# A fused layer on one core: the first stage's small adds and the feed-forward's factors are laid out anew over the engines

## The chip, the cores and the metric

The kernel runs on one core of one Trainium2 chip. The metric is the device time of one execution in microseconds (us), the median of several runs. The engines are called TensorE (PE; its weight loads are PEld), VectorE (DVE), ScalarE (ACT), GpSimd (POOL) and the sync queue (SP), which issues all transfers.

## The reference

For x of 2048 rows by 512, x plus an attention and a feed-forward, both of the normalized x:

```python
xn = (x - mean(x)) / sqrt(var(x) + 1e-5)
q = xn @ wq                       # 16 heads of 128 + 64
kva = xn @ wkv_a                  # 128 latents, 64 rotary key columns
ckv = kva[:, :128] * rsqrt(mean(kva[:, :128]**2) + 1e-6) * kv_norm_scale
k_nope, v = ckv @ wkv_b           # per head 128 and 128
scores = (concat(q_nope, rope(q_pe)) . concat(k_nope, rope(k_pe))) * 192**-0.5   # causal
attn = softmax(scores) @ v @ wo
mixed = sum_r(xn @ factors[r]) / sqrt(8) + bias    # 8 factors of 512x512
out = x + attn + mixed
```

## The kernel before

Every product is done in three matmuls of 16-bit high and low parts (`three`, L387 to L390). There are 16 row tiles of 128 rows (`NT`), 8 pairs of them (`NP`), 4 chunks of 512 queries (`NC`), and 64 units (`NU`): a chunk with a head each, the last chunk first. A unit has four rows r (query tiles); chunk 3, which the first 16 units work on, has four pieces of up to 512 keys per row.

Each engine has its own program in fixed order; semaphores bind them.

**First stage**, a loop over t = 0 to 19. On TensorE (L603 to L623): transpose of x tile t (`transpose_x`), some weight transposes, at odd t from 5 on `keys((t-5)/2)` (L475), which transposes a pair's scaled latents and turned rotary keys, `q_rope(0)` at t = 17 and `q_latent(0)` at t = 18, then `latent_product(t-2)`. On VectorE (L1203 to L1239), at even t from 4 on, `latent(p)` (L1043): the reciprocal (L1052), the rotary products out of the accumulator banks (L1055, L1058) into `kt` and `ktmp`, and the adds of the two halves (L1063), 128x128 each, two per pair. Later in the same t `value_parts` (L1066) subtracts the high part of the latents (128x256, L1069). It also takes the low parts of x, keys, absorbed weights, and the statistics of x. ScalarE (L822 to L857) normalizes, copies high parts, squares and takes roots; it scales the latents into `kt`, which has two buffers. GpSimd (L1334 to L1339) adds the eight factors into `fsum`, 28 adds of 128x512 in fixed order (`factor`, L1255), each when its tile has landed in one of four landing buffers, then scales some weights, adds the rotary halves of unit 0's queries (`q_rope`, L1295) and makes their low parts (`rope_parts`, L1309).

The sync queue is in order too (L1495 to L1530): x pairs, weights, 4 + 4 factor tiles, the rest of x, bias, table, then eight rounds of three factor tiles, where a load waits until GpSimd has used its buffer. In round 4 it also issues heads 2 and 3's weights; `load_wp(2)` waits for VectorE's `w_pe(0)` (L1022).

**Units.** TensorE writes a row's scores (L535 to L541; the rotary products L540, L541 wait for GpSimd's parts), VectorE takes the maxima (L1114, L1116) and the scaled negative maximum `nm` (L1132), ScalarE the exponentials (L769) and their high parts (L779), GpSimd the low parts (L1318), and a transposing transfer brings them to TensorE for the product with the latents. Between rows every engine does what the list `fills(i, r)` (L92) gives for this unit and row, each its own share of it. In unit 0 that list has: the query product of unit 1, the squares and norm of the factors (`sqf`, `nf`), their scaling to 16-bit parts (`factors_high` L811 on ScalarE, `factors_low` as the end of `scale_factors`, L971, on VectorE), and then all 8 feed-forward tiles, four in row 2 and four in row 3 (12 matmuls each). VectorE adds each tile into the residual (L1086) once GpSimd has added the bias to it (`add_bias`, L1276; two, three and three of them behind rows 0, 1 and 2).

```python
    if i == 0 and r >= 2:
        out += [("ffn", n) for n in range((r - 2) * QT, (r - 1) * QT)]
```

Small tiles of products rotate over four accumulator banks in the first stage and over three in the units (`bank_order`, L177): a use waits for the previous reader of its bank.

## Time and profile before

| | |
|---|---|
| median of 3 runs | 1557.49 us (1557.07 to 1558.05) |
| profiled execution, own time | 1555.18 us |
| its span | 1553.2 us |
| TensorE busy | 1483.4 us (96%) |
| VectorE busy | 1074.2 us (69%) |
| ScalarE busy | 971.6 us (63%) |
| GpSimd busy | 893.2 us (58%) |

The profile shows one execution. Times in it count from the span's start. A busy share over the whole span mixes the first stage (to about 85 us) with the 64 units, so the table by stage is to be read before the shares.

### The profile page before, as it was taken

To read this page: it belongs to the slowest core of one execution; us is meant where nothing else is said; L and a number is where in the kernel's file an instruction comes from. 1 tells how busy PE (TensorE), PEld (TensorE's weight loads), DVE (VectorE), ACT (ScalarE), POOL (GpSimd) and SP (SyncE) were. 2 spreads that over 40 slices of the span, in tenths; PEclk is the share of its full clock that TensorE was granted. 3 is DMA by queue.
4 is the path that set the end of the run, shared out by engine and by line. 5 is a ranking of instruction groups with operands and counts; after the bars stand their busy time and mean duration, and the time that the engine had idled before them with its cause. 6 is when DMAs were issued, how large, how long until landed. Compare 5 with 4: busy or idle time off the path is not lost.

```text
span 1553.2 us, 25687 instructions
## 1 busy us (share of the span) xinstructions
PE 1483.4 (96%) x7908; PEld 759.2 (49%) x7908; DVE 1074.2 (69%) x2534; ACT 971.6 (63%) x2409; POOL 893.2 (58%) x881
## 2 busy tenths in 40 slices
PE   4669999999999999999999999999999999999997
PEld 4534454545454455444454444544545555454543
DVE  6855778777877776665565655566766666686887
ACT  6654767677677767656666666665646665554554
POOL 3564566565556565656656565656646565564553
PEclk9979999999999999999999999999999999999999
DMA  8645777878777789878786777887856667754454
GB/s 274 193 115 118 152 158 137 162 154 166 151 153 155 139 152 195 154 130 168 144 164 138 135 142 144 150 166 130 180 129 133 136 139 151 153 127 98 107 127 106
DMA packets 646886, 229.93 MB, mean 148 GB/s; under 512 B 599392, under 2 KB 612192, under 8 KB 646112
## 3 DMA queue, kind: packets, MB, share of 16 engines
q1 hardware_dynamic: 646752, 228.30, 71.4%
q8 instruction: 65, 1.06, 0.3%
q14 instruction: 69, 0.57, 0.1%
HBM read 66.72 MB, written 18.87 MB: 55 GB/s over the span
## 4 chain that ended last, share of the span: by engine, by line
PE 83%; issue 5%; DVE 5%; ACT 4%; POOL 2%; DMA 1%; SPq 1%; DVEq 0%; ACTq 0%; POOLq 0%
PE ps L388 16%; PE ps L389 16%; PE ps L390 16%; PE ps L535 7%; PE ps L540 7%; PE ps L541 7%; PE ps L536 7%; PE ps L537 7%; ACT ex L769 2%; POOL early L1265 1%; DVE gm L1114 1%; DVE acc L1166 1%; DVE ps L1116 1%; DVE tot L900 0%; ACT wV L736 0%
## 5 line engine op out<-in xcount | busy, mean ns | idle before, releaser
L1318 POOL TENSOR_TENSOR st<-ex,st 128x512 f16<-128x512 f32 (+3 forms) x640 | 636.8, 1011 | 557.6 <-ACT st L779 545.9
L769 ACT ACTIVATE ex<-ps,nm,scales 128x512 f32<-128x512 f32 (+3 forms) x640 | 452.2, 709 | 504.6 <-DVE nm L1132 504.5
L1114 DVE TENSOR_REDUCE gm<-ps 128x1 f32<-128x512 f32 (+1 forms) x384 | 248.4, 668 | 166.9 <-PE ps L541 162.8
L779 ACT ACTIVATE st<-ex 128x512 f16<-128x512 f32 (+3 forms) x640 | 342.3, 562 | 5.9
L535 PE MATMUL ps<-kTh,q 128*128 128x512 f16 (+3 forms) x640 | 223.6, 349 | 8.3 <-DVE kRl L1078 4.3
L540 PE MATMUL ps<-kRh,q 128*128 128x512 f16 (+3 forms) x640 | 223.3, 349 | 3.3 <-POOL q L1309 3.3
L537 PE MATMUL ps<-kTh,q 128*128 128x512 f16 (+3 forms) x640 | 223.4, 349 | 0.0
L536 PE MATMUL ps<-kTl,q 128*128 128x512 f16 (+3 forms) x640 | 223.3, 349 | 0.0
L541 PE MATMUL ps<-kRl,q 128*128 128x512 f16 (+3 forms) x640 | 223.2, 349 | 0.0
L389 PE MATMUL ps<-pT,vH 128*128 128x512 f16 (+3 forms) x640 | 222.4, 347 | 0.0
L388 PE MATMUL ps<-pT,vH 128*128 128x512 f16 (+3 forms) x640 | 222.3, 347 | 0.0
L390 PE MATMUL ps<-pT,vL 128*128 128x512 f16 (+3 forms) x640 | 219.0, 347 | 0.0
L1166 DVE SCALAR_TENSOR_TENSOR acc<-ps,rden,acc 128x512 f32<-128x512 f32 x256 | 189.4, 742 | 3.0 <-PE ps L390 2.1
L1309 POOL TENSOR_TENSOR q<-rot,q 32x512 f16<-32x512 f32 x128 | 149.1, 1165 | 23.9 <-ACT q L758 11.9
L1116 DVE CUSTOM_DVE_ANT_0 ps<-ps,cmask 128x256 f32<-128x256 f32 (+3 forms) x256 | 132.6, 518 | 25.4 <-PE ps L541 22.8
L769 ACT ACTIVATION_READ_ACCUMULATOR ex<-ps,nm,scales 128x1 f32 x640 | 125.7, 196 | 0.0
L1091 DVE SCALAR_TENSOR_TENSOR q<-ps,q 128x512 f16<-128x512 f32 x64 | 44.1, 689 | 99.7 <-ACT q L752 99.6
L388 PE MATMUL ps<-wV,oT 128*128 128x512 f16 x256 | 97.0, 379 | 10.9 <-issue 9.5
L535 PEld LDWEIGHTS ps<-kTh,q 128*128 128x128 f16 x640 | 62.7, 98 | 75.2 <-ACT ex L769 8.7
L388 PE MATMUL ps<-xT,wA 128*128 128x512 f16 x256 | 97.1, 379 | 0.0
L389 PE MATMUL ps<-xT,wA 128*128 128x512 f16 x256 | 97.1, 379 | 0.0
L390 PE MATMUL ps<-xT,wA 128*128 128x512 f16 x256 | 97.1, 379 | 0.0
(202 smaller groups left out, 2197.8 us busy)
## 6 DMA issues: line engine op xcount, KB each, us to landing
wA<-w_abs SPq DMA_DIRECT2D x48, 256.0 KB, 2.9
wV<-w_vo SPq DMA_DIRECT2D x48, 256.0 KB, 2.9
pT<-st SPq DMA_TRANSPOSE x640, 3.2
early<-factors_in SPq DMA_DIRECT2D x32, 256.0 KB, 3.6
wP<-w_pe SPq DMA_DIRECT2D x24, 256.0 KB, 3.1
wsq<-wq_in SPq DMA_DIRECT2D x16, 256.0 KB, 3.9
wso<-wo_in SPq DMA_DIRECT2D x16, 256.0 KB, 3.1
w_abs<-wA SPq DMA_DIRECT2D x16, 256.0 KB, 2.6
```

Of the source, the lines that this page charges most:

```text
L388: e.matmul(o, a[0], b[0], start=first, stop=False)
L389: e.matmul(o, a[0], b[1], start=False, stop=False)
L390: return e.matmul(o, a[1], b[0], start=False, stop=last)
L535: e.matmul(b, q[:, i % 2, 0, qs], kTh[:, ks], start=True, stop=False)
L536: e.matmul(b, q[:, i % 2, 0, qs], kTl[:, ks], start=False, stop=False)
L537: e.matmul(b, q[:, i % 2, 1, qs], kTh[:, ks], start=False, stop=False)
L540: e.matmul(b, q[:, i % 2, 2, qs], kRh[:, ks], start=False, stop=False)
L541: e.matmul(b, q[:, i % 2, 2, qs], kRl[:, ks], start=False, stop=True).then_inc(z["p_s"], 1)
L769: e.activation(ex[:, n % NEX, 0:keys], s_bank(n)[:, 0:keys], ACT.Exp, bias=nm[:, (i * QT + r) % 4:(i * QT + r) % 4 + 1], scale=scales[:, p ...
L779: e.activation(stage(n, keys)[:, :, 0, :], ex[:, n % NEX, 0:keys].rearrange("p (t n) -> p t n", n=P), ACT.Copy).then_inc(z["a_pH"], 1)
L1114: e.tensor_reduce(m, b, AX_X, ALU.max).then_inc(z["v_max"], 1)
L1318: e.tensor_tensor(s[:, :, 1, :], ex[:, n % NEX, 0:keys].rearrange("p (t n) -> p t n", n=P), s[:, :, 0, :], ALU.subtract).then_inc(z["g_pL" ...
```

## The change

- The adds of the rotary halves of the keys and the split of the latents move from VectorE to GpSimd (`turned_keys`, `value_parts`), put between the factor adds: from the sixth factor add on, one after every fourth add, the other two adds later; what is left follows the weight scalings. `kt` and `ktmp` have four buffers instead of two and one.
- The squares, the norm and the high parts of the factors, and their low parts, move from unit 0 into the first stage. The squares of heads 2 and 3's weights stand behind unit 0's rotary parts on ScalarE.
- Unit 1's query product moves to the end of the first stage.
- The feed-forward tiles stand two behind each row of unit 0.
- The sync queue issues the key and value weights in round 1, and the query weights of heads 2 and 3 behind all factor tiles; the stores of x are later.

```diff
@@ -93,7 +93,7 @@
     if r == 0:
-        if i + 1 < NU:
+        if 1 <= i < NU - 1:
             out.append(("q", i + 1))
@@ -106,12 +106,10 @@
             out.append(("tq", i + 2))
-        if i == 0:
-            out += [("sqk", 2), ("sqf", 0)]
         if i // H == NC - 1 and i + 1 < NU and (i + 1) % H:
             out.append(("parts", i + 1))
-    if i == 0 and r >= 2:
-        out += [("ffn", n) for n in range((r - 2) * QT, (r - 1) * QT)]
+    if i == 0 and r == 0:
+        out += [("ffn", 0), ("ffn", 1)]
     for k in range(2, NC):
...
@@ -134,6 +130,8 @@
             out += [("sk", i + 3), ("sqp", i + 3)]
+    if i == 0 and r:
+        out += [("ffn", 2 * r), ("ffn", 2 * r + 1)]
     if r == 2 and i % 2 == 0 and i + 2 < H:
...
@@ -191,9 +189,11 @@
         if t == NT + 1:
-            pre.append(("pe", 0))
+            pre += [("pe", 0), ("nf", 0)]
         if t == NT + 2:
             pre.append(("q", 0))
+        if t == NT + 3:
+            pre.append(("q", 1))
     body = [k for i in range(NU + 2) for r in range(QT) for k in fills(i, r) if k[0] in IN_BANKS]
...
@@ -269,12 +270,12 @@
             ropen = stage_one.enter_context(nc.sbuf_tensor("ropen", [P, NT, 3, HALF], F32))
-            kt_sb = stage_one.enter_context(nc.sbuf_tensor("kt", [P, 2, 2, 2 * P], F32))
+            kt_sb = stage_one.enter_context(nc.sbuf_tensor("kt", [P, 4, 2, 2 * P], F32))
             biasb = bias_sb[:, :]
-            kt = [kt_sb[:, n, :, :] for n in range(2)]
+            kt = [kt_sb[:, n, :, :] for n in range(4)]
         wV = sb("wV", [P, 2, 2, E], F16)
         oT = sb("oT", [P, 2, CH], F16)
-        gap = sb("gap", [P, 3 * E], F32)
+        gap = sb("gap", [P, 5 * E], F32)
         with nc.sbuf_tensor("early", [P, 2, 4, 2, KE, CH], F16) as region:
...
@@ -474,9 +474,9 @@
                 b = free_bank(("kT", p2))
-                kk = kt[p2 % 2]
+                kk = kt[p2 % 4]
                 e.wait_ge(z["a_kk"], p2 + 1)
-                e.wait_ge(z["v_kk"], p2 + 1)
+                e.wait_ge(z["g_kk"], p2 + 1)
                 for i in range(2):
@@ -547,7 +547,7 @@
                 elif part.start == 0:
-                    e.wait_ge(z["v_vL"], NP)
+                    e.wait_ge(z["g_vL"], NP)
                 if part.start == 0 and i < H:
...
@@ -617,8 +615,11 @@
                     q_rope(0)
+                    norm(("nf", 0), ("a_sqf",), nrf[:, :])
                 if t == NT + 2:
                     q_latent(0)
+                if t == NT + 3:
+                    q_latent(1)
                 if 0 <= t - 2 < NT:
@@ -663,18 +664,18 @@
                 e.wait_ge(z["v_kva"], p2 + 1)
-                if p2 >= 2:
-                    e.wait_ge(z["p_kT"], p2 - 1)
-                    e.wait_ge(z["v_vL"], p2 - 1)
+                if p2 >= 4:
+                    e.wait_ge(z["p_kT"], p2 - 3)
+                    e.wait_ge(z["g_vL"], p2 - 3)
                 for i in range(2):
-                    ins = e.activation(kt[p2 % 2][:, i, 0:LORA], b[:, i, 0:LORA], ACT.Identity, bias=eps[:, 2:3],
+                    ins = e.activation(kt[p2 % 4][:, i, 0:LORA], b[:, i, 0:LORA], ACT.Identity, bias=eps[:, 2:3],
                                        scale=ssq[:, 2, 2 * p2 + i:2 * p2 + i + 1])
...
                 e.wait_ge(z["a_kk"], p2 + 1)
-                e.activation(vH[:, ts, :], kt[p2 % 2][:, :, 0:LORA], ACT.Copy).then_inc(z["a_vH"], 1)
+                e.activation(vH[:, ts, :], kt[p2 % 4][:, :, 0:LORA], ACT.Copy).then_inc(z["a_vH"], 1)
@@ -701,6 +702,8 @@
                     e.wait_ge(z["a_" + kind], i // 2)
+                if i == 2:
+                    e.wait_ge(z["a_sqf"], 1)
                 if i and kind == "sqk":
@@ -716,7 +719,7 @@
                 for kind in ("sqp", "sq0", "sq1", "sqk"):
-                    e.wait_ge(z["a_" + kind], 2)
+                    e.wait_ge(z["a_" + kind], 1)
                 square_sum(fsum.rearrange("p k n -> p (k n)"), 0, nrf[:, :]).then_inc(z["a_sqf"], 1)
@@ -797,14 +800,10 @@
                     w_pe(n)
-                elif kind == "nf":
-                    factors_high()
                 elif kind in ("sqp", "sq0", "sq1", "sqk"):
...
                     value_squares(kind, n)
-                elif kind == "sqf":
-                    factor_squares()
@@ -843,10 +842,9 @@
                 if t == NT:
-                    squares("sq0", 2)
-                    squares("sq1", 2)
-                if t == NT + 1:
-                    squares("sqp", 2)
+                    factor_squares()
+                if t == NT + 2:
+                    factors_high()
                 if t == NT + 3:
@@ -855,7 +853,10 @@
                     norm_scale(p + 2)
+            q_latent(1)
             rope_parts(0)
+            for kind in ("sqk", "sqp", "sq0", "sq1"):
+                squares(kind, 2)
             for i in range(NU + 2):
@@ -967,6 +968,8 @@
+            def factors_low():
                 e.wait_ge(z["a_ff"], 1)
@@ -1045,29 +1048,18 @@
                 halves = b[:, :, LORA:QH].rearrange("p t (a n) -> p t a n", a=2)
-                turned = kt[p2 % 2][:, :, P:2 * P].rearrange("p t (a d n) -> p t a d n", a=2, d=2)
+                turned = kt[p2 % 4][:, :, P:2 * P].rearrange("p t (a d n) -> p t a d n", a=2, d=2)
                 if p2 == 0:
...
                 e.reciprocal(ssq[:, 2, ts], ssq[:, 1, ts]).then_inc(z["v_rr"], 1)
-                if p2 >= 2:
-                    e.wait_ge(z["p_kT"], p2 - 1)
+                if p2 >= 4:
+                    e.wait_ge(z["p_kT"], p2 - 3)
                 e.tensor_tensor(turned[:, :, :, 0, :], halves, cos, ALU.mult)
...
-                    ins = e.tensor_tensor(ktmp[:, :, a, :], halves[:, :, 1 - a, :], ropen[:, ts, 1 + a, :], ALU.mult)
+                    ins = e.tensor_tensor(ktmp[:, p2 % 4, :, a, :], halves[:, :, 1 - a, :], ropen[:, ts, 1 + a, :], ALU.mult)
                 ins.then_inc(z["v_kva"], 1)
-                e.wait_ge(z["v_kva"], p2 + 1)
-                for d in (1, 0):
-                    ins = e.tensor_tensor(turned[:, :, :, d, :], turned[:, :, :, 0, :], ktmp, ALU.add)
-                ins.then_inc(z["v_kk"], 1)
-            def value_parts(p2):
-                ts = slice(2 * p2, 2 * p2 + 2)
-                e.wait_ge(z["a_vH"], p2 + 1)
-                e.tensor_tensor(vL[:, ts, :], kt[p2 % 2][:, :, 0:LORA], vH[:, ts, :], ALU.subtract).then_inc(
-                    z["v_vL"], 1)
...
@@ -1222,10 +1212,10 @@
                     w_abs(t // 3 - 3)
-                if t % 2 == 0 and 0 <= p - 2 < NP:
-                    value_parts(p - 2)
                 if t == 13:
                     w_pe(0)
+                if t == NT + 1:
+                    scale_factors()
                 if t == NT + 2:
@@ -1237,6 +1227,8 @@
                         norm_scale(p + 2)
+            q_latent(1)
+            factors_low()
             for i in range(NU + 2):
@@ -1264,6 +1256,21 @@
+            def value_parts(p2):
+                ts = slice(2 * p2, 2 * p2 + 2)
+                e.wait_ge(z["a_vH"], p2 + 1)
+                e.tensor_tensor(vL[:, ts, :], kt[p2 % 4][:, :, 0:LORA], vH[:, ts, :], ALU.subtract).then_inc(
+                    z["g_vL"], 1)
+            def turned_keys(p2):
+                turned = kt[p2 % 4][:, :, P:2 * P].rearrange("p t (a d n) -> p t a d n", a=2, d=2)
+                e.wait_ge(z["v_kva"], p2 + 1)
+                for d in (1, 0):
+                    ins = e.tensor_tensor(turned[:, :, :, d, :], turned[:, :, :, 0, :], ktmp[:, p2 % 4, :, :, :],
+                                          ALU.add)
+                ins.then_inc(z["g_kk"], 1)
@@ -1331,10 +1338,20 @@
             scale_keys(0)
+            turn, split = iter(range(NP)), iter(range(NP))
             for i in range(NF):
                 factor(i)
+                if i >= KE + 5 and (i - KE) % 4 == 1:
+                    turned_keys(next(turn))
+                if i >= KE + 5 and (i - KE) % 4 == 3:
+                    value_parts(next(split))
             scale_keys(2)
             scale_values(3)
+            for p2 in turn:
+                turned_keys(p2)
+                value_parts(next(split))
+            for p2 in split:
+                value_parts(p2)
             q_rope(0)
@@ -1515,14 +1532,16 @@
                     load_factor(i)
-                if n % 3 == 1:
-                    store_chunk(n // 3)
-                if n == 4:
-                    for m in range(2, 4):
-                        load_wk(m)
-                        load_wq(m)
-                    load_wp(2)
+                if n == 1:
+                    load_wk(2)
+                    load_wk(3)
                     load_wv(3)
+                if n in (4, 6):
+                    store_chunk(n // 2 - 2)
+            store_chunk(2)
+            for m in range(2, 4):
+                load_wq(m)
+            load_wp(2)
             load_wo(0)
```

## Rows read from the trace of the kernel before

**Rows 1.** Table by stage: stretch; length; busy (count) of PE, PEld, DVE, ACT, POOL; clock; DMA; GB/s.

```profile
50.00:60.00 10.00, 4.91 (x49) 4.05 (x49) 9.79 (x25) 5.13 (x16) 4.66 (x4) 1.00 0.67 217
60.00:70.00 10.00, 6.47 (x64) 5.63 (x64) 7.46 (x21) 8.24 (x24) 0.00 (x0) 1.00 0.30 65
77.65:84.90 7.25, 2.05 (x11) 0.89 (x10) 6.92 (x13) 2.62 (x7) 6.87 (x7) 0.79 0.91 338
84.90:93.90 9.00, 7.55 (x26) 3.07 (x27) 2.79 (x7) 1.66 (x2) 2.29 (x2) 0.60 0.07 25
93.90:101.70 7.80, 5.75 (x30) 2.78 (x28) 3.85 (x10) 7.71 (x19) 5.20 (x6) 1.00 0.38 72
101.70:115.70 14.00, 10.14 (x36) 4.66 (x37) 9.69 (x26) 8.02 (x17) 11.96 (x10) 0.77 0.45 88
300.00:600.00 300.00, 296.07 (x1593) 150.41 (x1590) 229.33 (x526) 211.99 (x535) 177.98 (x174) 1.00 0.78 153
```

**Rows 2.** Timeline of GpSimd: start us, us for all, what [idle before <- releaser].

```profile
18.11 4.94 POOL L1265 TENSOR_TENSOR early<-early 128x512 f32<-128x512 f32 x4 [6.97 <-DMA early<-factors_in]
33.91 7.38 POOL L1265 TENSOR_TENSOR early<-early 128x512 f32<-128x512 f32 x6 [10.86 <-DMA early<-factors_in]
...
82.36 0.61 POOL L1284 TENSOR_TENSOR wsk<-wsk,scl 128x256 f32<-128x256 f32 x1
82.93 0.39 POOL L1290 TENSOR_TENSOR wsv<-wsv,scl 128x128 f32<-128x128 f32 x1
```

**Rows 3.** Timeline of TensorE, same columns.

```profile
24.88 0.30 PE L481 MATMUL ps<-ident,kt 128*128 128x128 f32 x1 [0.50 <-ACT kt L670]
...
72.28 0.30 PE L481 MATMUL ps<-ident,kt 128*128 128x128 f32 x1 [2.54 <-DVE kt L1063]
...
87.78 0.61 PE L540 MATMUL ps<-kRh,q 128*128 128x512 f16 x1 [1.44 <-POOL q L1309]
...
148.95 0.38 PE L535 MATMUL ps<-kTh,q 128*128 128x512 f16 x1
```

**Rows 4.** Timeline of VectorE, same columns: the reciprocal that begins a pair.

```profile
29.66 0.16 DVE L1052 RECIPROCAL ssq<-ssq 128x2 f32<-128x2 f32 x1
...
40.01 0.15 DVE L1052 RECIPROCAL ssq<-ssq 128x2 f32<-128x2 f32 x1
...
58.52 0.16 DVE L1052 RECIPROCAL ssq<-ssq 128x2 f32<-128x2 f32 x1
...
65.59 0.15 DVE L1052 RECIPROCAL ssq<-ssq 128x2 f32<-128x2 f32 x1
...
69.92 0.17 DVE L1052 RECIPROCAL ssq<-ssq 128x2 f32<-128x2 f32 x1 [0.56 <-ACT ssq L659]
...
77.65 0.17 DVE L1052 RECIPROCAL ssq<-ssq 128x2 f32<-128x2 f32 x1 [2.67 <-ACT ssq L659]
```

**Rows 5.** Groups by shape, 0 to 85 us: count | busy us, mean ns | idle before.

```profile
L1063 DVE TENSOR_TENSOR kt<-kt,junk 128x128 f32<-128x128 f32 x16 | 8.2, 552 | 0.3
...
L1069 DVE TENSOR_TENSOR vL<-kt,vH 128x256 f16<-128x256 f32 x8 | 5.9, 736 | 0.9 <-ACT vH L677 0.9
```

**Rows 6.** Timelines of GpSimd, ScalarE, VectorE: rotary parts alone and beside factor work.

```profile
85.36 2.37 POOL L1309 TENSOR_TENSOR q<-rot,q 32x512 f16<-32x512 f32 x2 [0.74 <-ACT q L758]
...
107.63 2.09 ACT L811 ACTIVATE early<-early,eps,fsc 128x2048 f16<-128x2048 f32 x1
...
108.73 4.39 POOL L1309 TENSOR_TENSOR q<-rot,q 32x512 f16<-32x512 f32 x2
...
109.76 2.35 DVE L971 SCALAR_TENSOR_TENSOR early<-early,fsc 128x2048 f16<-128x2048 f32 x1 [3.91 <-ACT early L811]
```

**Rows 7.** Timelines of ScalarE and GpSimd, first row of unit 0.

```profile
93.93 0.78 ACT L769 ACTIVATE ex<-ps,nm,scales 128x512 f32<-128x512 f32 x1 [7.35 <-DVE nm L1132]
...
98.77 1.54 POOL L1318 TENSOR_TENSOR st<-ex,st 128x384 f16<-128x384 f32 x2 [0.28 <-ACT st L779]
100.27 2.49 POOL L1276 TENSOR_TENSOR acc<-acc,bias_all 128x512 f32<-128x512 f32 x2
```

More of the change, by code:

```diff
@@ L167, in fills @@
     return out
-IN_BANKS = ("q", "pe", "tkv", "wvo", "tq", "wabs", "out", "ffn", "nf")
+IN_BANKS = ("q", "pe", "tkv", "wvo", "tq", "wabs", "out", "ffn")
 SOON = {"nv": 0, "nrm": 1, "out": 2, "tq": 3, "q": 4}
@@ L248, in build @@
         junk = sb("junk", [P, CH], BF16)
+        ktmp = sb("ktmp", [P, 4, 2, 2, HALF], F32)
         gm = sb("gm", [P, 4, NC], F32)
@@ L305, in build @@
             "a_q", "a_parts", "a_o", "a_exp", "a_pH",
-            "v_wa", "v_bn", "v_var", "v_rstd", "v_nmr", "v_xt", "v_rr", "v_kva", "v_kk", "v_vL",
+            "v_wa", "v_bn", "v_var", "v_rstd", "v_nmr", "v_xt", "v_rr", "v_kva",
             "v_kT", "v_ff", "v_scl", "v_na", "v_aroot", "v_froot", "v_lat", "v_nf", "v_fsc", "v_nrm",
@@ L596, in fill @@
                     norm((kind, n), ("a_sqp", "a_sq0", "a_sq1", "a_r8"), nrm[:, :])
-                elif kind == "nf":
-                    norm((kind, n), ("a_sqf",), nrf[:, :])
                 elif kind == "nv":
```

8 lines of the change are left out of this document (1 added, 7 removed).

## The prediction, made before the run

> **What bounds the kernel now.** I read the table by stage first. From 300 us on, TensorE is busy 296 of 300 us [rows 1], so a change to the first stage can only move the moment at which that steady part begins. Before it the table shows a different limit: in 50:60 VectorE is busy 9.8 of 10 us and TensorE 4.9, in 77.65:84.9 TensorE works 2 of 7.25 us, and in 101.7:115.7 it is idle for almost 4 of 14. Second, the timeline of GpSimd [rows 2]: it adds the first four factor tiles from 18.1 us, has nothing until 33.91, when the fifth tile lands, and then adds them at 1.23 us each. Third, the chain of waits into the first scores: the product with the rotary keys starts at 87.78 [rows 3], released by GpSimd's parts of the query, and the first exponential is at 93.93 [rows 7], which I call T0. I call the eight groups of two x tiles pairs 0 to 7; `latent(p)` on VectorE begins each pair's keys with the reciprocal at L1052 [rows 4].
>
> **Part 1, the keys and latents go to GpSimd.** VectorE loses 16 adds of L1063 (8.2 us) and 8 subtractions of L1069 (5.9 us) [rows 5], 14.1 us of the engine that bounds the stage. GpSimd has not shown these shapes; its nearest rows are 0.39 us for 128x128 and 0.61 us for 128x256 [rows 2], so I take 0.8 us for the two adds of a pair (from 0.6, VectorE's pace when undisturbed, to 1.6, should the short runs of 32 cost double) and 0.6 for the split.
>
> The catch is where they stand in GpSimd's order: the first pair's add comes after the sixth factor tile. The fifth is not there before 33.91, and nothing ahead of it in the sync queue moved. So it ends at 33.91 + 2 x 1.23 + 0.8 = 37.2 us. TensorE wants it at 24.88 [rows 3]; `keys(0)` stands ahead of `latent_product(3)` in its order, and VectorE's `keys(0)` ahead of all its later work. So all three engines wait for some 12 us. From the transposes at 24.88 to `latent(1)` at 29.66 [rows 3, 4] were 4.8 us, about 1.2 of them two square sums on ScalarE that will now be done during the wait; TensorE restarts at half clock, which takes a little of that back, so 3.8: `latent(1)` at 41.0, 11.3 late.
>
> From there VectorE works through the old intervals [rows 4], less what was taken from it in each. Pair 1 to 2: 10.35 less 0.9, but the norm sums of `scale_pair` wait behind GpSimd's adds as before and the half clock of TensorE gives about 0.6 back, so 10.0: 51.0. Pairs 2 to 4: 18.5 less 4.3 = 14.2: 65.2. Pair 4 to 5: 7.1, paced by ScalarE, nothing gained: 72.3. Pair 5 to 6: 4.3: 76.6. GpSimd's own floor (four adds, 5.1, and 1.4 per pair) is 6.5 us a pair, with the first pair's add at 36.4, the second's at 42.7, thus 68.7 at pair 5, and isn't the bound. Pair 6 to 7: VectorE's part is ready at 77.2, GpSimd is then still at the last factors, two scalings and this add, ready about 78; before, `keys(6)` ran at 72.28 and `latent(7)` followed 5.4 us later [rows 3, 4]. With the factor norm (0.3) and a handover more: 84.2, against 77.65. **The first stage loses 6.6 us up to there.** The 4.7 us won back of 11.3 are what VectorE was relieved of where it was really the bound.
>
> **Part 2, the end of the stage.** Before, `latent(7)` to the rotary product took 87.78 - 77.65 = 10.1. After, ScalarE has in a row, from 84.8: latent scale and value parts 1.3, the scaled factors (2.1 for 128x2048 [rows 6]), and its short copies of 0.4 to 0.6 each (unit 0's queries, two of keys, unit 1's queries, the rotary parts: 2.4): 90.6. GpSimd's two parts take 2.4 [rows 6] alone. But VectorE's `factors_low` now runs just then: with it beside them the same two took 4.4 [rows 6]. I take 4.3: 94.9, that is 7.1 later than 87.78. The table load and the four squares of unit 2's weights on ScalarE fit before the first exponential, and unit 1's query product (12 matmuls, 2.6 us) fits while TensorE waits: both at nothing, unless ScalarE is the last, when they cost up to 2.4. TensorE has been busier just before, so it may be back at 2.4 GHz sooner than in 84.9:93.9, where the granted clock is 0.60 [rows 1], much of it at 1.2 GHz; from the rotary product to T0 were 6.15 us, at full clock it would be 4.1, I take 5: T0 = 99.9, **6.0 us later**.
>
> The Trainium skill (SBUF — State Buffer, "Who interferes with whom") says that a VectorE instruction with two SBUF inputs and a GpSimd one that reads SBUF block each other for the whole instruction; the rows agree (GpSimd's pair 4.4 against 2.4). The skill (GPSIMD Engine Reference, "Engine selection") calls GpSimd about twice as slow on two-input work; by that the first keys would be ready some 0.3 us later, while the rows here have 0.61 against 0.42.
>
> **Part 3, unit 0.** Before, from T0 to the second row of unit 1 are 148.95 - 93.93 = 55.0 us [rows 3, 7]; TensorE idles 5.9 of them (2.05 and 3.86 in the two stretches of [rows 1]) and does unit 1's queries (2.6) and the eight feed-forward tiles late and in a heap. After, two tiles stand behind each row, and VectorE adds each one in before the next row's maxima; it waits for GpSimd's bias sum, which stands behind GpSimd's low parts. Row 0: low parts end at T0 + 5.9 (6.4 before [rows 7], less 0.5 as the query copy is gone from ScalarE), two bias sums 2.5 [rows 7], the second tile's addition 0.75, maxima 2.9: row 1's exponentials at T0 + 12. Row 1: the norms and the query transpose on VectorE are hidden, since GpSimd is through its low parts after 6.9, then the rotary parts 2.4 and two bias sums 2.5, addition 0.75, maxima 3.1: T0 + 27.6. Row 2: low parts 6.7, one bias sum, addition and weights 2.8, maxima 3.1: T0 + 41.4. Unit 1's first scores then follow the four exponentials, 5.3: T0 + 46.8; its queries' successor and transposes 3.1: the second row starts at T0 + 50.0. **Unit 0 gains 5.0 us.** Queues: the stores of x wait for nothing new, the loads of unit 2's weights leave the factors' way and land before 80; both at nothing, hidden by the factor adds.
>
> **Sum.** +6.0 - 5.0 = +1.0 us. On the profiled execution's own 1555.2 that is 1556.2; the median shown is 2.3 above it, so I say 1558.5. A measurement of this kernel tells about 0.2% (3.1 us) from nothing: no change.
>
> **Rivals.**
> 1. The late first keys are absorbed, faster. If VectorE, 14.1 us lighter, runs up to GpSimd's floor, `latent(7)` comes 4 us earlier; and should the factor subtraction get between GpSimd's two parts without holding them, 2 more: 1558.5 - 6 = 1552.5. For it: VectorE at 9.8 of 10 in 50:60. Against: in 60:70 it is down to 7.5 of 10 [rows 1]. Chance 0.24.
> 2. Factor adds hold up the keys, slower. GpSimd's stream is in order, and a pair's add can find a 1.3 us factor add ahead of it; TensorE and VectorE then wait at each pair. Six pairs by up to 1.3 less my slack come to some 5 us; it decides as soon as GpSimd's period (6.5) lies above VectorE's interval, which is so for pairs 5 to 6 (4.3). L1022 and L895, undisturbed in 55:70 before, would also meet GpSimd's adds. 1563.5. Chance 0.24.
> 3. The spread tiles save nothing, slower: if TensorE's waits of 3 to 4 us before the fourth tile and before row 3 let its clock fall, as 84.9:93.9 shows after a wait (granted clock 0.60 [rows 1]), the 5.0 of part 3 shrink to about 1: 1562.5. Chance 0.10.
> 4. The change does not reach the end at all (both parts hidden by the same chain): 1557.5, inside the forecast's case.
>
> **Numbers.** The forecast's case (with 4) has 0.42: own range 1555 to 1561. Low end: 1552.5 less 1.5 for the bounds of GpSimd's price; high end: 1563.5 plus 2.5 for ScalarE as the last of the stage, a little over. Faster 0.24, same 0.42, slower 0.34.
>
> **What would show it.** Right: GpSimd's first rotary add at about 36.4 us, the transposes of `keys(0)` at 37 and a hole of 11 to 12 us before them on TensorE, ScalarE and VectorE; `latent(7)` near 84; T0 near 100; GpSimd's two rotary parts at over 4 us; no heap of TensorE's feed-forward tiles after row 3, and 50 us from T0 to unit 1's second row. Wrong: `keys(0)` before 34 us, T0 before 95 or after 104, or a feed-forward addition of VectorE that does not wait for the bias.

## The result, and the profile after

The changed kernel takes 1562.76 us (median of 8 runs, 1560.18 to 1564.16) against 1557.28 (8 runs, 1556.49 to 1558.42) on the same chip: ratio 1.0034 [1.0024, 1.0043], 5.5 us slower. The profiled execution has a span of 1561.7 us, its own time is 1564.07, 8.9 above the profiled execution of before (1555.18); before's lies 2.1 under its median and this one 1.3 above.

The table by stage of the changed kernel (columns as in [rows 1]); the first and the last stretch are new here, before had 9.25, 11.29 and 11.68 us busy on PE, DVE and ACT in the first, and PE 10.00 at clock 1.00 in the last.

```profile
24.00:37.00 13.00, 0.63 (x4) 0.39 (x4) 2.96 (x8) 3.85 (x10) 2.28 (x2) 0.71 0.73 230
...
50.00:60.00 10.00, 6.89 (x56) 6.14 (x56) 9.75 (x33) 5.74 (x17) 7.30 (x9) 0.83 0.60 196
60.00:70.00 10.00, 6.60 (x66) 5.60 (x67) 7.52 (x21) 7.92 (x21) 8.88 (x11) 1.00 0.76 252
84.90:93.90 9.00, 7.69 (x42) 3.54 (x40) 6.04 (x19) 6.73 (x16) 3.08 (x5) 1.00 0.01 2
93.90:101.70 7.80, 3.71 (x11) 1.48 (x12) 4.22 (x3) 3.62 (x10) 3.95 (x2) 0.78 0.00 1
101.70:115.70 14.00, 13.25 (x71) 6.64 (x68) 5.78 (x17) 4.65 (x13) 6.22 (x6) 1.00 0.32 63
300.00:600.00 300.00, 296.09 (x1590) 150.29 (x1589) 228.63 (x519) 211.88 (x536) 179.36 (x175) 1.00 0.79 153
1355.00:1365.00 10.00, 8.63 (x38) 4.04 (x39) 4.80 (x10) 4.38 (x11) 6.19 (x7) 0.83 0.84 149
```

The steady part is as before (296.09 against 296.07 of 300 [rows 1]). In 24:37 three engines do almost nothing. The timelines show who holds them: GpSimd, TensorE, ScalarE, VectorE of the changed kernel, in this order.

```profile
34.72 2.48 POOL L1257 TENSOR_TENSOR early<-early 128x512 f32<-128x512 f32 x2 [11.24 <-DMA early<-factors_in]
37.16 0.86 POOL L1270 TENSOR_TENSOR kt<-kt,ktmp 128x128 f32<-128x128 f32 x2
...
38.17 0.45 PE L481 MATMUL ps<-ident,kt 128*128 128x128 f32 x1 [13.54 <-POOL kt L1270]
...
39.29 0.38 ACT L684 ACTIVATE kTh<-ps 128x256 f16<-128x256 f32 x1 [11.41 <-PE ps L482]
...
39.98 0.42 DVE L1068 SCALAR_TENSOR_TENSOR kTl<-ps,kTh 128x256 f16<-128x256 f32 x1 [12.60 <-ACT kRh L685]
...
43.49 0.15 DVE L1055 RECIPROCAL ssq<-ssq 128x2 f32<-128x2 f32 x1
51.95 0.16 DVE L1055 RECIPROCAL ssq<-ssq 128x2 f32<-128x2 f32 x1
58.98 0.15 DVE L1055 RECIPROCAL ssq<-ssq 128x2 f32<-128x2 f32 x1
66.49 0.16 DVE L1055 RECIPROCAL ssq<-ssq 128x2 f32<-128x2 f32 x1
...
72.24 1.88 DVE L1025 SCALAR_TENSOR_TENSOR wP<-wsp,scales,wP 128x512 f16<-128x512 f32 x1
74.71 0.15 DVE L1055 RECIPROCAL ssq<-ssq 128x2 f32<-128x2 f32 x1
79.75 0.17 DVE L1055 RECIPROCAL ssq<-ssq 128x2 f32<-128x2 f32 x1 [1.25 <-ACT ssq L660]
86.96 0.17 DVE L1055 RECIPROCAL ssq<-ssq 128x2 f32<-128x2 f32 x1 [0.69 <-ACT ssq L660]
```

GpSimd sits idle for 11.24 us, for a factor tile that has not landed, with the first keys' add behind it in its order. TensorE's 13.54, ScalarE's 11.41 and VectorE's 12.60 us of idle time are this one wait, handed on. `latent(1)` comes 13.8 us later than before [rows 4], `latent(7)` still 9.3 later. The end of the stage, the same timelines:

```profile
93.63 4.30 POOL L1316 TENSOR_TENSOR q<-rot,q 32x512 f16<-32x512 f32 x2 [2.70 <-ACT q L761]
...
93.67 3.25 DVE L974 SCALAR_TENSOR_TENSOR early<-early,fsc 128x2048 f16<-128x2048 f32 x1
...
97.99 0.61 PE L540 MATMUL ps<-kRh,q 128*128 128x512 f16 x1 [4.18 <-POOL q L1316]
...
103.34 0.22 DVE L1124 SCALAR_TENSOR_TENSOR nm<-rm,scales,head 128x1 f32<-128x1 f32 x1
...
103.59 0.78 ACT L772 ACTIVATE ex<-ps,nm,scales 128x512 f32<-128x512 f32 x1 [5.99 <-DVE nm L1124]
```

And unit 0 on VectorE: each row's first feed-forward addition waits some 7.4 us for GpSimd's bias sum, and the next row's `nm` stands behind it.

```profile
110.97 0.75 DVE L1078 SCALAR_TENSOR_TENSOR acc<-ps,fsc,acc 128x512 f32<-128x512 f32 x1 [7.42 <-POOL acc L1283]
...
115.38 0.22 DVE L1124 SCALAR_TENSOR_TENSOR nm<-rm,scales,head 128x1 f32<-128x1 f32 x1
126.46 0.75 DVE L1078 SCALAR_TENSOR_TENSOR acc<-ps,fsc,acc 128x512 f32<-128x512 f32 x1 [7.33 <-POOL acc L1283]
...
139.26 0.75 DVE L1078 SCALAR_TENSOR_TENSOR acc<-ps,fsc,acc 128x512 f32<-128x512 f32 x1 [7.39 <-POOL acc L1283]
```

To compare kernels I use five marks, all starts of instructions of VectorE: `latent(0)`, which moves only with the landing of x, and the 1st, 6th, 12th and 200th `nm` of VectorE (one per row of keys and unit; L1132 before, L1124 after). The 6th is the second row of unit 1, the 200th lies in unit 49. The column from nm 1 to 6 is called the unit 0 column. There is one profiled execution per kernel, and the changed kernel was profiled twice (k9_again is the same program): its `latent(0)` to nm 1 was 79.9 and 81.1, its unit 0 column 56.1 both times. So about 1 us of difference in the first of these columns says nothing.

| kernel | median us | ratio [95%] | latent(1) | latent(0) to nm 1 | nm 1 to 6 | nm 6 to 12 | nm 12 to 200 |
|---|---|---|---|---|---|---|---|
| before | 1557.28 | | 29.7 | 70.5 | 60.6 | 50.3 | 1170.9 |
| changed | 1562.76 | 1.0034 [1.0024, 1.0043] | 43.5 | 79.9 | 56.1 | 51.9 | 1172.5 |
| k1_vector | 1558.64 | 1.0005 [0.9994, 1.0017] | 30.7 | 78.7 | 56.1 | 50.4 | 1170.8 |
| k2_first | 1561.22 | 1.0019 [1.0007, 1.0032] | 30.4 | 77.7 | 56.1 | 52.0 | 1172.5 |
| k3_early | 1555.77 | 0.9983 [0.9972, 0.9994] | 30.4 | 73.3 | 56.1 | 52.5 | 1172.5 |
| k4_heap | 1561.00 | 1.0013 [1.0002, 1.0024] | 44.1 | 81.7 | 54.5 | 50.3 | 1172.5 |
| k5_lock | 1561.61 | 1.0026 [1.0014, 1.0038] | 44.1 | 78.5 | 56.1 | 50.4 | 1170.8 |
| k6_bias | 1556.26 | 0.9991 [0.9981, 1.0001] | 44.2 | 80.4 | 48.8 | 50.3 | 1170.8 |
| k7_queue | 1556.15 | 0.9988 [0.9979, 0.9996] | 30.6 | 70.6 | 58.9 | 50.3 | 1170.9 |
| k8_three | 1543.73 | 0.9910 [0.9895, 0.9926] | 30.5 | 68.6 | 49.3 | 50.4 | 1171.0 |
| k9_again | 1564.55 | 1.0039 [1.0027, 1.0051] | 43.9 | 81.1 | 56.1 | 52.3 | 1172.6 |
| k10_late | 1543.09 | 0.9899 [0.9885, 0.9913] | 30.2 | 68.5 | 48.9 | 50.3 | 1172.5 |
| k11_heap | 1548.86 | 0.9939 [0.9925, 0.9953] | 30.9 | 68.3 | 52.1 | 50.3 | 1170.8 |
| k12_query | 1561.14 | 1.0022 [1.0012, 1.0033] | 43.9 | 79.1 | 56.4 | 50.5 | 1170.8 |

Against before the changed kernel loses 9.4 in the first stage, wins 4.5 in unit 0, and loses 1.6 and again 1.6 far behind it: 8.1 of the 8.9 us between the two profiled executions (0.2 more is the landing of x). The last two columns take one of two values, and I come back to them.

### The profile page after: what moved, and what is told of

The parts are those of the page before. It is cut to its first block, busy times and chain, and to the rows that moved or that the text cites. A ratio compares the mean times of both kernels' runs of the same rounds, so it can differ in the third digit from the quotient of the medians.

```text
span 1561.7 us, 25688 instructions
## 1 busy us (share of the span) xinstructions
PE 1486.5 (95%) x7908; PEld 760.7 (49%) x7908; DVE 1064.4 (68%) x2510; ACT 971.8 (62%) x2409; POOL 904.3 (58%) x905
## 4 chain that ended last, share of the span: by engine, by line
PE 81%; DVE 6%; issue 4%; POOL 4%; ACT 4%; DMA 1%; SPq 1%; DVEq 0%; ACTq 0%; POOLq 0%
PE ps L388 16%; PE ps L389 16%; PE ps L390 16%; PE ps L535 7%; PE ps L540 7%; PE ps L541 6%; PE ps L536 6%; PE ps L537 6%; ACT ex L772 2%; POOL early L1257 2%; DVE gm L1106 1%; DVE ps L1108 1%; POOL st L1325 1%; DVE acc L1158 1%; POOL q L1316 1%
## 5 line engine op out<-in xcount | busy, mean ns | idle before, releaser
L1083 DVE SCALAR_TENSOR_TENSOR q<-ps,q 128x512 f16<-128x512 f32 x64 | 44.1, 689 | 99.6 <-ACT q L755 99.6
```

## The experiments

Ratios are against the kernel before on the same chip (medians 1558.15, 1558.13 and 1558.38 in three groups: k1 to k4, k5 to k8, k9 to k12). Diffs are against the changed kernel unless another is named. Of two kernels in different groups the ratios are compared; where a difference of medians is given across groups, the chips differ by up to 1.1 us.

**k1_vector: the moved adds and splits go back to VectorE**, all else as changed.

```diff
@@ VectorE, latent(p)
                 ins.then_inc(z["v_kva"], 1)
+                e.wait_ge(z["v_kva"], p2 + 1)
+                for d in (1, 0):
+                    ins = e.tensor_tensor(turned[:, :, :, d, :], turned[:, :, :, 0, :], ktmp[:, p2 % 4, :, :, :],
+                                          ALU.add)
+                ins.then_inc(z["g_kk"], 1)
...
@@ GpSimd, between the factor adds
-                if i >= KE + 5 and (i - KE) % 4 == 1:
-                    turned_keys(next(turn))
-                if i >= KE + 5 and (i - KE) % 4 == 3:
-                    value_parts(next(split))
```

> The changed kernel with one part undone: the rotary adds and the latent splits are back on VectorE, at their old places; all else as changed. Theory A (the adds stand too late in GpSimd's order and cost more than VectorE's relief gives): no hole of 12 us at the first pair, latent(7) at about 79 us instead of 87.0, first exponential near 95 instead of 103.6, time about 1554.5 (8 us below the changed kernel, about 3 below the kernel before). Rival B (the loss comes from the factor work, unit 1's queries and their waits at the stage's end): the first stage still ends 6 us or more later than in the kernel before, time 1560 or more.

Measured 1558.64, 0.29% below the changed kernel's ratio, some 4.5 us. The hole is gone (`latent(1)` at 30.7), yet 8.2 of the 9.4 us of the first stage stay: `latent(7)` is at 83.4 and the first exponential at 103.3, where theory A had 79 and 95. So both theories hold in part: the late adds cost time, and rival B's stage, 6 us or more too long without them, is there as well, though not its 1560. The timelines of VectorE and GpSimd in k1 show what the adds cost on VectorE:

```profile
41.18 2.07 DVE L1065 TENSOR_TENSOR kt<-kt,ktmp 128x128 f32<-128x128 f32 x2
...
45.86 1.43 DVE L1072 TENSOR_TENSOR vL<-kt,vH 128x256 f16<-128x256 f32 x1
...
43.29 11.35 POOL L1270 TENSOR_TENSOR early<-early 128x512 f32<-128x512 f32 x9 [0.19 <-DMA early<-factors_in]
```

Two adds that GpSimd does in 0.86 us take VectorE 2.07 beside factor adds, each nearly as long as a factor add (1.24). The kernel before had that too, so it isn't what makes the stage of k1 longer than before. The durations of the two lines there, from the view of one line's instructions, minimum, median and maximum in ns:

```profile
L1063 DVE TENSOR_TENSOR kt<-kt,junk x16: 278/291/1358, 23.9 to 78.5; 128x128 f32<-128x128 f32 x16
...
L1069 DVE TENSOR_TENSOR vL<-kt,vH x8: 414/426/1494, 25.3 to 79.8; 128x256 f16<-128x256 f32 x8
```

At the medians they are 16 x 0.29 + 8 x 0.43 = 8.1 us of the 14.1 of [rows 5]; the other 6 were time in which VectorE was held. With them on VectorE `latent(7)` comes 59.0 us after `latent(0)`, against 63.5 in the changed kernel and 54.4 before. The end of the stage is slower instead (19.6 from `latent(7)` to nm 1 against 16.4). By nm 1 the two are only 1.2 apart, no more than the two profiles of the changed kernel; 3.2 more of their difference is in the last two columns.

What keeps the stage long can be read against k7 below, the kernel before with the new queue order: beside that order, k1 has the factor work and unit 1's queries in the first stage, the spread tiles and the larger buffers. From `latent(0)` to `latent(7)` it takes 59.0 against 56.5, from there to the rotary product 14.2 against 8.9, in unit 0 56.1 against 58.9. So what moved out of unit 0 put some 8 us into the stage and, with the waits for the bias, took only 2.8 out of unit 0.

**k2_first: only the first pair's add and split come early**, the others at their places.

```diff
-                if i >= KE + 5 and (i - KE) % 4 == 1:
+                for _ in range([3, 9, 13, 17, 21, 25].count(i - KE)):
...
-                if i >= KE + 5 and (i - KE) % 4 == 3:
+                for _ in range([7, 11, 15, 19, 23, 27].count(i - KE)):
```

> The changed kernel, with only the first pair's rotary add moved ahead: after the fourth factor add (which ends at 23.5 us) instead of after the sixth; pairs 1 to 7 as changed. Theory A: the first hole goes, but pair 1's add still stands behind the sixth tile of the late batch, at about 42 us where TensorE wants it at 31, so about half is won back: latent(2) at 47 instead of 52.0, time about 1557.5. Rival A2 (only the one hole at the first pair counts, later adds are in time): all 12 us of the hole come back, time about 1552. Rival B: no more than 2 us, time 1561 or more.

Measured 1561.22, by its number rival B's case. But `latent(1)` is at 30.4 and `latent(2)` only at 49.4: the hole moved on to the second pair, whose add stood behind the same tiles (TensorE in k2):

```profile
44.12 0.45 PE L481 MATMUL ps<-ident,kt 128*128 128x128 f32 x1 [12.33 <-POOL kt L1270]
```

**k3_early: the first two pairs before the tile that is late**, the third after six more adds.

```diff
-                if i >= KE + 5 and (i - KE) % 4 == 1:
+                if i == KE + 3:
+                    for p2 in range(2):
+                        turned_keys(next(turn))
+                        value_parts(next(split))
+                if i >= KE + 9 and (i - KE) % 4 == 1:
...
-                if i >= KE + 5 and (i - KE) % 4 == 3:
+                if i >= KE + 11 and (i - KE) % 4 == 3:
```

> The changed kernel, with the rotary adds and splits of pairs 0 and 1 both ahead of the late factor tiles (after the fourth factor add), pair 2's add after the tenth, later pairs as changed. Theory A: no hole over 3 us before 40 us on TensorE, latent(2) at about 39 instead of 52.0, latent(7) at 77 instead of 87.0 (GpSimd's 6.5 us a pair and the factor squares become the floor), first exponential near 93.5, time about 1552.5, below the kernel before by about 5 us. Rival B: the time stays above 1560.

Measured 1555.77, 7.0 below the changed kernel (7.9 by the ratios) and 0.17% below before, 3.3 above what I expected. The stage is 6.5 us shorter (73.3 against 79.9), the unit 0 column equal, the two late losses both there. So the place of the first adds alone costs what the median lost, and more. Against k1, which has them on VectorE, 5.3 us of the stage: that is what the move is worth when it is put better. It isn't put well yet: the third pair's add still stands behind six factor adds, and TensorE waits 6.12 us for it, in k8 5.57. Timelines of GpSimd and TensorE in k3:

```profile
24.80 0.86 POOL L1270 TENSOR_TENSOR kt<-kt,ktmp 128x128 f32<-128x128 f32 x2 [0.62 <-DVE ktmp L1061]
...
31.13 0.86 POOL L1270 TENSOR_TENSOR kt<-kt,ktmp 128x128 f32<-128x128 f32 x2 [4.37 <-DVE ktmp L1061]
...
35.65 7.38 POOL L1257 TENSOR_TENSOR early<-early 128x512 f32<-128x512 f32 x6 [2.44 <-DMA early<-factors_in]
42.98 0.86 POOL L1270 TENSOR_TENSOR kt<-kt,ktmp 128x128 f32<-128x128 f32 x2
...
43.99 0.45 PE L481 MATMUL ps<-ident,kt 128*128 128x128 f32 x1 [6.12 <-POOL kt L1270]
...
91.11 0.61 PE L540 MATMUL ps<-kRh,q 128*128 128x512 f16 x1 [4.21 <-POOL q L1316]
```

**k4_heap: the feed-forward tiles in two heaps again.**

```diff
-    if i == 0 and r == 0:
-        out += [("ffn", 0), ("ffn", 1)]
+    if i == 0 and r >= 2:
+        out += [("ffn", n) for n in range((r - 2) * QT, (r - 1) * QT)]
...
-    if i == 0 and r:
-        out += [("ffn", 2 * r), ("ffn", 2 * r + 1)]
```

> The changed kernel with the feed-forward tiles as before: four behind row 2 and four behind row 3 of unit 0; all else as changed. Theory C (the spreading gains nothing: what unit 0 won is the query product and the factor work that left it, and the spread tiles bring VectorE three waits of 7 us for the bias): time within 1.5 us of the changed kernel, 1561 to 1564. Rival D (the spreading is what won the 5 us of unit 0): 3 to 5 us above the changed kernel, 1566 to 1568.

Measured 1561.00, as theory C had it. Unit 0 takes 54.5, not 56.1: spread as they are, the tiles cost 1.6 us more than in heaps, and the 4.5 us won in unit 0 are 6.1 from the factor work and the queries that left it, less this 1.6.

**k5_lock: `factors_low` one step earlier on VectorE**, out of GpSimd's way.

```diff
+                    factors_low()
...
-            factors_low()
```

> The changed kernel with VectorE's low parts of the factors moved one step earlier, ahead of unit 0's queries, so that they no longer run beside GpSimd's two rotary parts. Theory L (the two block each other): the two rotary parts take 2.4 us instead of 4.3, the rotary product and the first exponential come 2.0 us earlier, time 2 us below the changed kernel (about 0.22% above the kernel before instead of 0.35%). Rival: the first exponential doesn't move, because VectorE now hands over unit 0's queries and keys 2.4 us later.

Measured 1561.61. GpSimd's timeline:

```profile
95.08 2.37 POOL L1316 TENSOR_TENSOR q<-rot,q 32x512 f16<-32x512 f32 x2 [2.69 <-ACT q L761]
```

2.37 instead of 4.30 us, and from `latent(7)` to the rotary product 9.1 us instead of 11.0, which k2, k3, k4, k6 and k9 have as well: the 1.9 us are on the path. By the median it is 1.2 us.

**k6_bias: four bias sums before unit 0**, the others two behind each of rows 0 and 1.

```diff
-        out += [("bias", n) for n in range(2 * QT) if min((n + 1) // 3, 2) == r]
+        out += [("bias", n) for n in range(QT, 2 * QT) if (n - QT) // 2 == r]
...
+            for n in range(QT):
+                add_bias(n)
```

> The changed kernel with four of GpSimd's bias sums before unit 0 and two behind each of its rows 0 and 1, so that no feed-forward addition waits for one. Theory C (the spread tiles gain nothing because VectorE waits for the bias sum behind each row): the three waits of 7.4 us on VectorE go, TensorE becomes the bound of unit 0, from the first negative maximum to that of unit 1's second row 51 us instead of 56.1, time 5 us below the changed kernel, level with the kernel before. Rival: TensorE's own work fills unit 0 anyway, at most 1 us.

Measured 1556.26, 6.5 below the changed kernel; unit 0 takes 48.8 instead of 56.1, 2 us better than expected. GpSimd makes the sums while it would be idle, and the additions wait for TensorE's product instead (GpSimd and VectorE in k6):

```profile
98.91 4.93 POOL L1283 TENSOR_TENSOR acc<-acc,bias_all 128x512 f32<-128x512 f32 x4
...
105.96 0.75 DVE L1078 SCALAR_TENSOR_TENSOR acc<-ps,fsc,acc 128x512 f32<-128x512 f32 x1 [1.65 <-PE ps L390]
...
113.10 0.22 DVE L1124 SCALAR_TENSOR_TENSOR nm<-rm,scales,head 128x1 f32<-128x1 f32 x1
```

The second row's maxima come 9.0 us after the first's instead of 12.0.

**k7_queue: the kernel before with the new order of the sync queue alone** (diff against the kernel before).

```diff
-                if n % 3 == 1:
-                    store_chunk(n // 3)
-                if n == 4:
-                    for m in range(2, 4):
-                        load_wk(m)
-                        load_wq(m)
-                    load_wp(2)
+                if n == 1:
+                    load_wk(2)
+                    load_wk(3)
...
+                if n in (4, 6):
+                    store_chunk(n // 2 - 2)
+            store_chunk(2)
+            for m in range(2, 4):
+                load_wq(m)
+            load_wp(2)
```

> The kernel before with one part of the change alone: the order of the sync queue. Heads 2 and 3's weights no longer hold up the last nine factor tiles, so GpSimd adds them from 55 us on instead of from 70.6. Theory Q (GpSimd's adds block VectorE's instructions with two inputs in SBUF, and in the kernel before the blocked queue happened to keep them out of the stretch in which VectorE is the bound): latent(7) 3 to 5 us later, time 2 to 4 us above the kernel before. Rival (the factors are only ready earlier): the first rotary product comes earlier since GpSimd is free for it, time 0 to 1 us below the kernel before.

Measured 1556.15, 0.12% [0.04, 0.21] faster. My theory of a loss fell. GpSimd's factor adds do crowd together in k7,

```profile
43.22 11.37 POOL L1265 TENSOR_TENSOR early<-early 128x512 f32<-128x512 f32 x9 [0.27 <-DMA early<-factors_in]
56.43 7.44 POOL L1265 TENSOR_TENSOR early<-early 128x512 f32<-128x512 f32 x6 [1.84 <-DMA early<-factors_in]
```

and `latent(7)` comes 2.1 us later after `latent(0)` (56.5 against 54.4), but nm 1 does not (70.6 against 70.5), and unit 0 is 1.7 shorter. The rival had the right side, but not its way: the rotary product comes 0.8 us later after `latent(0)`, not earlier.

**k8_three: k3, k5 and k6 together.**

```diff
@@ VectorE
+                    factors_low()
...
@@ GpSimd
+                if i == KE + 3:
+                    for p2 in range(2):
+                        turned_keys(next(turn))
+                        value_parts(next(split))
...
+            for n in range(QT):
+                add_bias(n)
```

> The changed kernel with three repairs together: the rotary adds of pairs 0 and 1 ahead of the late factor tiles (as in the run before), the factors' low parts one step earlier, and the bias sums ahead. If the three causes are separate, their gains add: 8 us of the first, 2 of the second, 5 of the third below the changed kernel, thus 8 to 10 us below the kernel before (ratio 0.994 to 0.995). If one hides another, the ratio stays above 0.996.

Measured 1543.73 (4 runs, 1543.33 to 1543.95), 0.9910 [0.9895, 0.9926]: 14 us below before and 19 below the change, more than I expected. From `latent(0)` to nm 6 are 117.9 us against 131.0 before and 136.0 after. Of that the parts alone gave 6.5 (k3), 7.3 (k6) and 1.9 (k5), 15.7; the rest is at the stage's end, where `latent(7)` to nm 1 takes 12.9 us against 17.4 in k3. Of these 4.5 us, 1.9 are GpSimd's two parts. The other 2.5 are TensorE's clock: it writes the first row's scores, from the rotary product to nm 1, in 3.8 us at a granted clock of 1.00, in k3 in 6.3 at 0.59, behind a wait of 4.21 us. k11, without the early bias sums, has the 3.8 at 1.00 too. But k5, behind waits as short as k8's (2.36 and 0.49 us), has 5.4 at 0.70, so what keeps the clock up is open. TensorE, VectorE and GpSimd in k8:

```profile
89.06 0.39 PE L540 MATMUL ps<-kRh,q 128*128 128x512 f16 x1 [0.49 <-POOL q L1316]
...
79.96 0.17 DVE L1055 RECIPROCAL ssq<-ssq 128x2 f32<-128x2 f32 x1 [0.69 <-ACT ssq L660]
...
86.62 2.37 POOL L1316 TENSOR_TENSOR q<-rot,q 32x512 f16<-32x512 f32 x2 [2.70 <-ACT q L761]
...
92.85 1.17 DVE L1124 SCALAR_TENSOR_TENSOR nm<-rm,scales,head 128x1 f32<-128x1 f32 x1
101.87 0.72 DVE L1124 SCALAR_TENSOR_TENSOR nm<-rm,scales,head 128x1 f32<-128x1 f32 x1
```

The first `nm` takes 1.17 us instead of 0.22, until GpSimd's early bias sums end at 94.01, and the first exponential waits for it: 94.06, where k11 has 93.12. This 1 us, which the early sums cost, is in the unit 0 column (49.3).

**k9_again: the changed kernel itself**, in the group of k10 to k12.

> The changed kernel itself, once more, beside the other runs of this call. Its profile showed, beyond the first stage and unit 0, 1.6 us lost in units 1 and 2 (a wait of 1.5 us for ScalarE's squares, granted clock 0.83 in 180 to 190 us) and 1.9 us at unit 48 (clock 0.83 in 1355 to 1365). If these belong to the kernel, they are in this profile too and the time is 5 to 6 us above the kernel before. If they are chance, one or both are missing and the medians lie 3 to 5 us apart.

1564.55, 1.0039 [1.0027, 1.0051]. The unit 0 column repeats, the two late losses too, within 0.4 and 0.1 us. The stage does not: it is 1.2 us longer, 0.9 of it between the rotary product and nm 1, where the granted clock is 0.60 and was 0.70.

**k10_late: k8 with the factors' squares, norm and low parts one to two steps later** (diff against k8), since in k3 VectorE's norm scale stood 6.43 us in wait for the squares.

```diff
-            pre += [("pe", 0), ("nf", 0)]
+            pre.append(("pe", 0))
...
-            pre.append(("q", 0))
+            pre += [("nf", 0), ("q", 0)]
...
-                if t == NT:
-                    factor_squares()
-                if t == NT + 2:
-                    factors_high()
...
+                if t == NT + 1:
+                    factor_squares()
...
+            factors_high()
...
@@ VectorE
-                if t == NT + 1:
-                    scale_factors()
...
+                    scale_factors()
...
-                    factors_low()
...
+            factors_low()
```

> The kernel with the rotary adds of pairs 0 and 1 and the bias sums early, and the factor work ordered anew: the squares on ScalarE between keys(6) and latent(7), the norm on TensorE behind the last latent product, the high parts behind unit 0's rotary parts and unit 1's queries, the low parts last. Theory F (the factor work in the first stage lies on the way to the first rotary product, as the norm holds up latent(7) by 1.3 us and the high parts the queries by 2.1): first rotary product 3 us earlier than with the three repairs, first negative maximum near 90.3 instead of 92.8 us, ratio 0.989 to 0.990 against 0.991 for the three. Rival (VectorE's low parts then delay the first maxima): no gain, ratio 0.991 or more.

Measured 1543.09, as k8. The rotary parts come 2.4 us earlier (84.26 against 86.62), nm 1 only 0.4 (92.42 against 92.85): the factors' low parts, now at the end, hold the first maxima. The ratio of 0.9899 is the number of theory F, but the mark it rests on (nm 1 at 90.3) did not come, and the intervals of k8 and k10 overlap.

**k11_heap: k8 with the heaps and the bias sums as they were** (diff against k8).

```diff
-    if i == 0 and r == 0:
-        out += [("ffn", 0), ("ffn", 1)]
+    if i == 0 and r >= 2:
+        out += [("ffn", n) for n in range((r - 2) * QT, (r - 1) * QT)]
...
-    if i == 0 and r:
-        out += [("ffn", 2 * r), ("ffn", 2 * r + 1)]
...
-        out += [("bias", n) for n in range(QT, 2 * QT) if (n - QT) // 2 == r]
+        out += [("bias", n) for n in range(2 * QT) if min((n + 1) // 3, 2) == r]
```

> The kernel with the rotary adds of pairs 0 and 1 early, the factors' low parts one step earlier, and the feed-forward tiles as before in heaps of four behind rows 2 and 3, with the bias sums where they were. Theory C (spreading pays only if the bias sums are out of the way; in heaps unit 0 took 54.5 us to unit 1's second row, spread 56.1, spread with early bias sums 48.8): first negative maximum near 93 us, ratio 0.995 to 0.996, 5 to 6 us above the three repairs. Rival (heaps are as good once the stage is repaired): ratio 0.992 or less.

Measured 1548.86, 5.1 above k8 by medians, 2.8 in the unit 0 column (52.1 against 49.3). So spreading with early sums wins 3 to 5 us over heaps; without them it lost 1.6. k11 changes the place of the sums together with the tiles, but in its heaps no addition waits for a sum: the waits are of at most 1.84 us, for TensorE's products.

**k12_query: unit 1's queries go back to unit 0.**

```diff
-        if 1 <= i < NU - 1:
+        if i + 1 < NU:
...
-        if t == NT + 3:
-            pre.append(("q", 1))
...
-                if t == NT + 3:
-                    q_latent(1)
...
-            q_latent(1)
```

> The changed kernel with unit 1's queries back behind row 0 of unit 0, ahead of the feed-forward tiles. Theory: the 2.6 us product fits into TensorE's waits at either place (it waits in unit 0 for VectorE, which waits for the bias sums), so the time is within 1 us of the changed kernel; the stage ends up to 0.7 us earlier, since ScalarE's copy no longer stands ahead of the rotary parts. Rival (it was on the path of unit 0 as in the kernel before): 2.5 us above the changed kernel.

Measured 1561.14, 3.4 below k9 and 1.6 below the first measurement of the changed kernel: neither the theory nor the rival had that. GpSimd's rotary parts wait less for ScalarE, whose copy of unit 1's queries stood ahead of unit 0's rotary copy:

```profile
93.02 4.31 POOL L1310 TENSOR_TENSOR q<-rot,q 32x512 f16<-32x512 f32 x2 [1.55 <-ACT q L757]
```

1.55 against 2.70 us (the changed kernel and k9), and `latent(7)` to the rotary product is 9.9 against 11.0 in both, so 1.1 of the 3.4 is shown. The rest coincides with the last two columns, where k12 has no late loss.

## Why the prediction was right or wrong

1562.76 lies in the range of 1551 to 1566, but 4.3 us above the forecast: "no change" did not come, the slower side with its 0.34 did. That the range held is partly luck. The two profiled executions are 8.9 us apart where +1.0 was forecast, and 3.1 of that, the two late losses, has no term in the sum and no rival. The number lies next to those of rivals 3 (1562.5) and 2 (1563.5), but neither's mechanism made it. Step by step:

**The hole at the first pair: right.** GpSimd's first rotary add was foreseen at 36.4 and is at 37.16, the transposes at 37.2 and 38.17, the hole at some 12 us on three engines. The cause is shown by k2 and k3: the hole moves to the second pair, then to the third, as the adds move ahead of the tiles.

**`latent(1)` at 41.0: mis-sized by 2.5.** It is at 43.49. The tile landed 0.8 us later than before (34.72 against 33.91 [rows 2]), the transposes followed 0.2 later than I had, and from the transposes to `latent(1)` went 5.3 us instead of 3.8: I had said that the half clock "takes a little of that back". TensorE restarts with rows of 0.45 and 0.42 us where it had 0.30, at a granted clock of 0.50 from 37 to 41, and goes on at 0.37 per matmul instead of 0.25 to 0.27 until 43.1. It works without a pause from 38.17 until then, so this is where the 1.5 go.

**Pairs 1 to 7: right in sum.** From `latent(1)` to `latent(7)` I had 43.2 and measured 43.5. Pair 1 to 2 was 1.5 shorter than mine, pair 4 to 5 1.1 longer (8.2, "paced by ScalarE, nothing gained") and pair 5 to 6 0.7: in pair 4, L1025 takes 1.88 instead of 0.74 us (L1022 before), since GpSimd now adds through it. I had named this instruction in rival 2 without a price. That rival's own mechanism, a factor add ahead of a pair's add, did not come: GpSimd stood idle before the adds of pairs 1 to 7, for VectorE's product, as in these two of its timeline.

```profile
52.64 0.86 POOL L1270 TENSOR_TENSOR kt<-kt,ktmp 128x128 f32<-128x128 f32 x2 [2.08 <-DVE ktmp L1061]
...
75.39 0.86 POOL L1270 TENSOR_TENSOR kt<-kt,ktmp 128x128 f32<-128x128 f32 x2 [1.81 <-DVE ktmp L1061]
```

Its side and the meeting with L1025 were right, its main reason was not. Rival 1 needed VectorE to run up to GpSimd's floor; it did not either, with 9.75 of 10 us busy in 50:60.

**The end of the stage: right in kind, 0.9 short.** `latent(7)` to the rotary product 11.0 (10.7), from there to the first exponential 5.6 (5.0). That the two rotary parts would take 4.3 beside VectorE's factor work was right (4.30), and k5 shows that it lies on the path, as k12 shows of the queries, "both at nothing, unless ScalarE is the last": it is the last, for about 1.1 us. Together T0 is 9.7 later instead of 6.0. **This sum is the step that was mis-sized**: 2.5 of the 3.7 missing are the term of `latent(1)`, 0.3 the pairs, 0.9 the end.

**Unit 0: right.** I had T0 + 12, 27.6 and 41.4 for the next rows and 50.0 for the second row of unit 1; measured 12.0, 27.65, 41.6 and 49.6, with the three waits for the bias. The 5.0 us of gain are 5.4 by this last mark and 4.5 by nm 6. They don't come from the spreading, though, as k4 shows. Rival 3's cause came, its price did not: TensorE waits before the fourth tile, its matmuls then take 0.61 us instead of 0.39, and the granted clock is 0.83 in 115:125 (1.00 in 101.7:115.7). The rows come when foreseen all the same, for VectorE waits for the bias then.

```profile
118.54 0.61 PE L388 MATMUL ps<-early 128*128 128x512 f16 x1 [2.76 <-DVE wX L986]
```

**Behind unit 0: "+1.0" was taken to stay as it is.** It did not: 1.6 us are lost in units 1 and 2 and 1.6 at unit 48. The queue's new order, "both at nothing", has a share in the first where it occurs. ScalarE's squares of head 3's query weights, which are now loaded last, wait for their transfer, and TensorE for them (ScalarE and TensorE of the changed kernel):

```profile
184.74 0.63 ACT L692 ACTIVATE sqr<-wsq 128x512 bf16<-128x512 f32 x1 [1.05 <-DMA wsq<-wq_in]
...
185.72 0.36 PE L437 MATMUL ps<-nrm,ones 128*128 128x4 f32 x2 [1.53 <-ACT sqr L692]
...
1356.37 0.23 PE L540 MATMUL ps<-kRh,q 128*128 128x128 f16 x1 [2.08 <-POOL q L1316]
```

At unit 48 TensorE waits 2.08 us for rotary parts; the kernel before waits 1.84 there as well. What differs is the clock afterwards: 0.83 in 1355:1365, while it stayed 1.00 before. What sets it is open. In single profiled executions the first loss is in four kernels (changed, k2, k3, k9), the second in those and in k4 and k10; k5, nearly the same program as the changed one, has neither. The first goes with the wait: in the four kernels that have it TensorE waits 1.49 to 1.63 us for these squares and its clock falls, in the others no wait there is above 0.9. The second does not: TensorE waits 2.08 us at that place in k5, k6, k8, k11 and k12 too, and its clock stays up. Since the runs of the changed kernel spread over 4 us and those of k9 over 4.8, the second may be a matter of the execution. I did not test it.

**What each part is worth**, from the runs: the factor work and the queries put some 8 us into the stage (k1 against k7); the move to GpSimd as placed costs 4.5 us by the median against VectorE, of which the marks up to nm 1 show only 1.2, within their noise, and with the first two adds early it wins 5.3 in the stage; the waits for the bias cost 6.5 to 7.3; the lock at the rotary parts 1.2 to 1.9; the queries at the stage's end 1.1 and up to 3.4; the queue's order gives back 2. With the three places mended (k8) the same change gains 14 us.

## What to carry to other kernels

Before giving an in-order engine a small new task, look at what its next instruction waits for: a 0.9 us add behind a tile that lands 11 us later stops every engine that needs it, while in front of that tile it costs nothing. The same holds for a sum that a consumer needs soon (the bias): make it in the engine's idle time, ahead of the row, and only then spread the work that depends on it. And compare an instruction's least and median time with its mean before taking a busy engine for a working one: of the 14.1 us moved off VectorE 8.1 were work, the rest was time held by GpSimd, and an instruction that stayed (L1025) was held in their place.
